# Order of outputs and splitting of inputs in the shared-key attention stage of a decoder kernel

## The reference

```python
def _L1_attn_ref(x, proj_q, proj_k, proj_v, proj_o):
    Q = jnp.einsum('bnd,hdk->bhnk', x, proj_q)
    K = jnp.einsum('bmd,dk->bmk', x, proj_k)
    V = jnp.einsum('bmd,dv->bmv', x, proj_v)
    logits = jnp.einsum('bhnk,bmk->bhnm', Q, K)
    weights = jax.nn.softmax(logits, axis=-1)
    O = jnp.einsum('bhnm,bmv->bhnv', weights, V)
    Y = jnp.einsum('bhnv,hdv->bnd', O, proj_o)
    return Y
x = x + _L1_attn_ref(_layernorm(x, axis=-1), ...)
```

## Time and profile before

| what | us |
|---|---|
| median of the runs | 1040.63 |
| the profiled execution, its time | 1041.43 |
| its span, first to last instruction | 1039.6 |
| TensorE busy in it (88% of the span) | 915.1 |
| VectorE, ScalarE, GpSimd busy | 669.2, 503.6, 326.6 |
| shared-key stage, from the first instruction to the last before the next stage | 498.0 to 748.4 |
| first scores of the loop | 523.63 |
| the stage after it and the rest | 748.4 to 1039.6 |

### The profile page before, as it was taken

The page is one execution under the profiler, slowest core; times in us unless marked ns, Lnnn a source line. Parts: engine busy times, 40 slices in busy tenths (PEclk is TensorE's granted clock), DMA queues, the critical chain, the costliest instruction groups (busy, mean ns, idle before and its releaser), DMA issues. The chain is left out here.

```text
span 1039.6 us, 13450 instructions
## 1 busy us (share of the span) xinstructions
PE 915.1 (88%) x4354; PEld 506.9 (49%) x4354; DVE 669.2 (64%) x1367; ACT 503.6 (48%) x997; POOL 326.6 (31%) x329
## 2 busy tenths in 40 slices
PE   5888889999999986999688888888897999878996
PEld 2445535333332243567566777677542333344565
DVE  5856659888889534354565555655479999444654
ACT  3886445777777740121254444444312777533421
POOL 7236536100000001365154444445131000015933
PEclk9999989999999995899898888988999999969999
DMA  5040054022228307532300000000010352056200
GB/s 149 1 152 1 0 85 77 1 48 47 48 60 257 103 1 250 221 115 91 112 1 0 1 1 1 1 1 1 21 57 3 116 191 81 1 211 211 82 17 26
DMA packets 41657, 73.83 MB, mean 71 GB/s; under 512 B 8964, under 2 KB 27780, under 8 KB 40436
## 3 DMA queue, kind: packets, MB, share of 16 engines
q1 hardware_dynamic: 36372, 59.68, 18.9%
q0 software_dynamic: 4400, 13.11, 4.0%
q10 hardware_dynamic: 816, 0.17, 0.1%
HBM read 49.67 MB, written 10.49 MB: 58 GB/s over the span
## 5 line engine op out<-in xcount | busy, mean ns | idle before, releaser
L1081 DVE TENSOR_REDUCE c_amx<-PS 128x1 f32<-128x512 f32 x256 | 159.0, 682 | 27.7 <-PE PS L981 27.5
L1174 ACT ACTIVATE c_aE<-PS 128x512 f32<-128x512 f32 x256 | 132.5, 603 | 47.1 <-PE PS L993 46.9
L1861 POOL TENSOR_SCALAR s_Pn<-s_Pr,s_rs 128x512 f32<-128x512 f32 x64 | 100.1, 1567 | 122.3 <-DVE s_rs L1903 122.0
L72 POOL TENSOR_SCALAR rstd<-mv 128x4 f32<-128x4 f32 x8 | 1.9, 232 | 337.8 <-DVE mv L95 337.7
L981 PE MATMUL PS<-c_aKs,c_aQs 99*128 99x512 bf16 x256 | 96.6, 388 | 5.1 <-DMA c_aQs<-area 3.6
L993 PE MATMUL PS<-c_aQs,c_aKs 99*128 99x512 bf16 x256 | 94.5, 380 | 3.5 <-ACT c_aE L1174 2.3
L1894 DVE TENSOR_REDUCE s_mx<-PS 128x1 f32<-128x512 f32 x64 | 44.0, 688 | 82.1 <-PE PS L2005 82.1
L1992 ACT ACTIVATE s_Pr<-PS,s_nmx 128x512 f32<-128x512 f32 x64 | 44.1, 689 | 107.8 <-DVE s_nmx L1896 107.5
L1081 DVE TENSOR_REDUCE h_amx<-PS 128x1 f32<-128x512 f32 x128 | 79.3, 682 | 8.4 <-PE PS L981 8.2
L1174 ACT ACTIVATE h_aE<-PS 128x512 f32<-128x512 f32 x128 | 67.5, 601 | 21.6 <-PE PS L993 21.2
L1004 PE MATMUL PS<-c_aE,c_VB 128*17 128x512 f32 x512 | 67.4, 598 | 0.1
(11 more groups left out here) (495 smaller groups left out, 1994.6 us busy)
## 6 DMA issues: line engine op xcount, KB each, us to landing
area<-in_e_w SPq DMA_DIRECT2D x16, 512.0 KB, 9.9
area<-in_g_w SPq DMA_DIRECT2D x8, 1024.0 KB, 6.7
c_aKs<-area SPq DMA_DIRECT2D x48, 128.0 KB
g_B<-in_g_b SPq DMA_DIRECT2D x1, 4096.0 KB, 14.2
c_aQs<-area SPq DMA_DIRECT2D x48, 64.0 KB
h_aQs<-h_QP SPq DMA_DIRECT2D x48, 64.0 KB
early<-in_ctxT SPq DMA_DIRECT2D x2, 1024.0 KB, 7.0
e_B<-in_e_b SPq DMA_DIRECT2D x1, 2048.0 KB
```

The source lines that it names most:

```text
L1081: dve.tensor_reduce(self.mx[:, qt, j, half:half + 1], PS[:, n % MB, :], AX.X, ALU.max).then_inc(self.max_done, 1)
L1174: act.activation(self.E[kt % 2][:, j, :], PS[:, MB + x % XB, :], ACT.Exp, scale=0.25).then_inc(self.exp_done, 1)
L1861: pool.tensor_scalar(Pn[g % NPB][:, :], Pr[g % NPB][:, :], rs[:, g % NPB:g % NPB + 1], None, ALU.mult).then_inc(pn_ready, 1)
```

## The change

Outputs are issued one step later against the transposes, projections two steps later, and the loop has two more steps. VectorE makes the low part of a finished output last in its step and no longer first. In the head, ScalarE copies the transposed input unsplit (XT); TensorE makes keys, values and the queries of the first unit from unsplit f32 operands, one matmul where there were three, and the values move into the loop's first four steps, a pair of row tiles in each. VectorE copies the high parts of the input and of all query weights, GpSimd makes their low parts, the query weights head by head; VectorE makes the low parts of wo head by head in the first eight steps. The parts of wk and wv are gone.

```diff
-    STEPS = G + 2 * TB + LAG + 1
+    STEPS = G + 2 * TB + LAG + 3
     def output_part(g):
 
-        v, m = divmod(g - LAG, TB)
+        v, m = divmod(g - LAG - 1, TB)
         return v - 1, m
 
     def projection_part(g):
 
-        v, i = divmod(g - LAG - 1, TB)
+        v, i = divmod(g - LAG - 3, TB)
         return v - 2, i
...
     def kv_bank(n):
-        return PS[:, 4 + n % 4, :] if n < B else PS[:, 4 + n % 4, 0:2 * DK].rearrange("p (i c) -> p i c", i=2)
+        return PS[:, 5 + n, :] if n < B else PS[:, 7 - n % 2, 0:2 * DK].rearrange("p (i c) -> p i c", i=2)
...
+    def wq_count(h):
+        return h if h > 0 else H
...
-            pool.wait_ge(wqh_ready, 1)
-            pool.tensor_tensor(wqs[1][:, :, :, :], wq[:, :, :, :], wqs[0][:, :, :, :].bitcast(F32),
-                               ALU.subtract).then_inc(wq_ready, 1)
+            def low_weights(h):
+                pool.tensor_tensor(wqs[1][:, h, :, :], wq[:, h, :, :], wqs[0][:, h, :, :].bitcast(F32),
+                                   ALU.subtract).then_inc(wq_ready, 1)
+
+            def low_input(g):
+                b, k = divmod(g, KD)
+                cols = slice(b * S, (b + 1) * S)
+                pool.wait_ge(xh_ready, g + 1)
+                pool.tensor_tensor(XTs[1][:, k, cols], XT[:, k, cols], XTs[0][:, k, cols].bitcast(F32),
+                                   ALU.subtract).then_inc(xl_ready, 1)
+
+            pool.wait_ge(wh_ready, 1)
+            low_weights(1)
+            for g in range(KD):
+                low_input(g)
+            for h in range(2, H):
+                low_weights(h)
+            low_weights(0)
+            for g in range(KD, KD * B):
+                low_input(g)
...
-            for w, parts in ((wk, wks), (wv, wvs)):
-                dve.tensor_copy(parts[0][:, :, :], w[:, :, :]).then_inc(wh_ready, 1)
+            dve.tensor_copy(wqs[0][:, :, :, :], wq[:, :, :, :]).then_inc(wh_ready, 1)
             dve.tensor_copy(wos[0][:, :, :], wo[:, :, :]).then_inc(wh_ready, 1)
-            dve.wait_ge(wh_ready, 2)
-            for w, parts in ((wk, wks), (wv, wvs)):
-                dve.tensor_tensor(parts[1][:, :, :], w[:, :, :], parts[0][:, :, :].bitcast(F32),
-                                  ALU.subtract).then_inc(w_ready, 1)
-            dve.wait_ge(wh_ready, 3)
-            dve.tensor_tensor(wos[1][:, :, :], wo[:, :, :], wos[0][:, :, :].bitcast(F32),
-                              ALU.subtract).then_inc(w_ready, 1)
             for g in range(KD * B):
                 b, k = divmod(g, KD)
                 cols = slice(b * S, (b + 1) * S)
-                dve.wait_ge(xkvh_ready, g + 1)
-                dve.tensor_tensor(XTs[1][:, k, cols], PS[:, g, :], XTs[0][:, k, cols].bitcast(F32),
-                                  ALU.subtract).then_inc(xkv_ready, 1)
-            for n in range(NKV):
+                dve.wait_ge(xf_ready, g + 1)
+                dve.tensor_copy(XTs[0][:, k, cols], XT[:, k, cols]).then_inc(xh_ready, 1)
+
+            def low_kv(n):
                 high, low = kv_parts(n)
-                dve.wait_ge(xkvh_ready, KD * B + n + 1)
-                dve.tensor_tensor(low, kv_bank(n), high.bitcast(F32), ALU.subtract).then_inc(xkv_ready, 1)
+                dve.wait_ge(kvh_ready, n + 1)
+                dve.tensor_tensor(low, kv_bank(n), high.bitcast(F32), ALU.subtract).then_inc(kv_ready, 1)
+
+            def low_projection(h):
+                dve.wait_ge(wh_ready, 2)
+                dve.tensor_tensor(wos[1][:, h, :], wo[:, h, :], wos[0][:, h, :].bitcast(F32),
+                                  ALU.subtract).then_inc(wo_ready, 1)
+
+            for b in range(B):
+                low_kv(b)
 
...
             low_queries(0)
             for g in range(STEPS):
                 n, qt = divmod(g, TB)
-                v, m = output_part(g - 1)
-                if 0 <= v < UN and m == TB - 1:
-                    low_output(v)
                 if g < G:
                     maximum(g)
                 if 1 <= g <= G:
                     inverse_sum(g - 1)
                 if 0 <= g - LAG - 1 < G:
                     low_transposes(g - LAG - 1)
+                if 1 <= g <= VP:
+                    low_kv(B + g - 1)
                 if qt == 2 and n + 1 < UN:
                     low_queries(n + 1)
-                if (g - LAG - 1) % TB == TB - 1 and (g - LAG - 1) // TB - 2 == H - 1:
+                if g < H:
+                    low_projection(g)
+                v, m = output_part(g - 1)
+                if 0 <= v < UN and m == TB - 1:
+                    low_output(v)
+                if projection_part(g) == (H - 1, TB - 1):
                     take_output(0)
...
-            act.activation(wqs[0][:, :, :, :], wq[:, :, :, :], ACT.Copy).then_inc(wqh_ready, 1)
             for g in range(KD * B):
                 b, k = divmod(g, KD)
                 act.wait_ge(xT_done, g + 1)
-                act.activation(XTs[0][:, k, b * S:(b + 1) * S], PS[:, g, :], ACT.Copy).then_inc(xkvh_ready, 1)
-            for n in range(NKV):
+                act.activation(XT[:, k, b * S:(b + 1) * S], PS[:, g, :], ACT.Copy).then_inc(xf_ready, 1)
+
+            def take_kv(n):
                 act.wait_ge(kv_mm, n + 1)
-                act.activation(kv_parts(n)[0], kv_bank(n), ACT.Copy).then_inc(xkvh_ready, 1)
+                act.activation(kv_parts(n)[0], kv_bank(n), ACT.Copy).then_inc(kvh_ready, 1)
+
+            for b in range(B):
+                take_kv(b)
 
...
+                if g < VP:
+                    take_kv(B + g)
...
-            pe.wait_ge(w_ready, 2)
             for b in range(B):
-                pe.wait_ge(xkv_ready, KD * (b + 1))
+                pe.wait_ge(xf_ready, KD * (b + 1))
                 for k in range(KD):
-                    last = products(PS[:, 4 + b, :], [w[:, k, :] for w in wks], [x[:, k, b * S:(b + 1) * S] for x in XTs],
-                                    k == 0, k == KD - 1)
+                    last = pe.matmul(PS[:, 5 + b, :], wk[:, k, :], XT[:, k, b * S:(b + 1) * S],
+                                     start=(k == 0), stop=(k == KD - 1))
                 last.then_inc(kv_mm, 1)
-            for i in range(0, NT, 2):
-                n = B + i // 2
-                if n >= 4:
-                    pe.wait_ge(xkv_ready, KD * B + n - 3)
+            for k in range(KD):
+                last = pe.matmul(PS[:, 4, :], wq[:, 0, k, :], XT[:, k, 0:S], start=(k == 0), stop=(k == KD - 1))
+            last.then_inc(q_mm, 1)
+
+            def values(i):
+
+                n = B + i
+                pe.wait_ge(kv_ready, n - 1 if i >= 2 else B)
                 for j in range(2):
+                    t = 2 * i + j
                     for k in range(KD):
-                        last = products(PS[:, 4 + n % 4, j * DK:(j + 1) * DK],
-                                        [x[:, k, (i + j) * P:(i + j + 1) * P] for x in XTs], [w[:, k, :] for w in wvs],
-                                        k == 0, k == KD - 1)
+                        last = pe.matmul(PS[:, 7 - n % 2, j * DK:(j + 1) * DK], XT[:, k, t * P:(t + 1) * P],
+                                         wv[:, k, :], start=(k == 0), stop=(k == KD - 1), skip_group_check=True)
                 last.then_inc(kv_mm, 1)
-            pe.wait_ge(xkv_ready, KD * B + NKV)
-            pe.wait_ge(wq_ready, 1)
-            pe.wait_ge(w_ready, 3)
 
             def query_part(n, k):
                 b, h = divmod(n, H)
-                if n >= 1 and k == 0:
+                if k == 0:
                     pe.wait_ge(q_ready, n)
+                    pe.wait_ge(xl_ready, KD * (b + 1))
+                    pe.wait_ge(wq_ready, wq_count(h))
                 last = products(PS[:, 4, :], [w[:, h, k, :] for w in wqs], [x[:, k, b * S:(b + 1) * S] for x in XTs],
                                 k == 0, k == KD - 1)
...
                 pe.wait_ge(q_ready, n + 1)
+                pe.wait_ge(kv_ready, b + 1)
...
                 if m == 0:
+                    pe.wait_ge(kv_ready, B + VP)
                     pe.wait_ge(pt_ready, (n + 1) * TB)
...
                     pe.wait_ge(o_ready, n + 1)
+                    pe.wait_ge(wo_ready, H)
...
-            for k in range(KD):
-                query_part(0, k)
             for g in range(STEPS):
                 n, qt = divmod(g, TB)
                 if g < G:
                     scores(g)
+                if g < VP:
+                    values(g)
```

More of the change, by code:

```diff
@@ L1819, in shared_kv_stage @@
     XTs, KTs, Vs = split("XT", [P, KD, T]), split("KT", [P, T]), split("V", [P, NT, DK])
-    wks, wvs = split("wk", [P, KD, DK]), split("wv", [P, KD, DK])
     QT, OT = ([split(f"{name}{n}", [P, S]) for n in range(2)] for name in ("QT", "OT"))
@@ L1825, in shared_kv_stage @@
     mx, nmx, sm, rs = (sb(n, [P, NPB]) for n in ("mx", "nmx", "sm", "rs"))
-    wqh_ready, wq_ready, wh_ready, w_ready = (sem(n) for n in ("wqh_ready", "wq_ready", "wh_ready", "w_ready"))
```

(8 more changed lines are left out.)

## The result

The changed kernel takes 1006.19 us (median of 4 runs, 1004.0 to 1010.64) against 1040.35 us (1037.04 to 1044.63) for the one before: a ratio of 0.9675, with a 95% interval of 0.9626 to 0.9723, and 34 us less. The forecast was 999 us, 42 us less.

A forecast was written before the change was run, and what follows sets the result against it. TensorE was taken to bound the stage, losing time to waits on VectorE's low transposes and half clock behind them. Gains 28.2 + 13.1 + 2.4 - 1.7 = 42.0 us off 1040.63 gave 999; range 992 to 1004, 8-in-10 992 to 1018.

The forecast's parts named there:

- steps 1 and 2: Each unit's output: new wait of 1.37 us in place of 2.07, clock stays full behind it, unit 11.5 us.
- step 3: The 13 units from the output of head 1 to that of head 14: 148.8 us against 177.0, 28.2 gained.
- steps 4 and 5: Head and first eight loop steps: scores begin 15.5 us earlier, of which 13.1 us stay at head 1's output.
- step 6: Tail, up to the last projection: 13.7 us against 16.06, 2.4 us gained.
- step 7: TensorE resting before the first scores and thinly loaded in two early loop steps: one half-clock stretch, 1.7 us, given back.
- A: First steps: GpSimd's normalisation holds VectorE's low projection weights, 2.9 us a step instead of 1.95, time 1006; chance 0.12.
- B: Units: the clock still falls at each new wait, 13.2 us a unit, time 1020; chance 0.12.
- C: Every unit: clock falls and does not return within the next stretch; slower, 1064 us with three such stretches; chance 0.04.
- D: Head's conversions and small differences collide, or the o_ready wait is as long as the old one; some 1008; chance 0.10.

## Why the prediction was right, and where not

1. *The new wait (steps 1 and 2).* Right. It was to be ended by the low output at about 1.1 to 1.2 us as the view shows idle time. It was, at 1.20 us, and the clock stayed at 1.00 behind it, with 2.20 of 3.40 us busy (forecast 2.3). The kernel with the low output first shows that its place in VectorE's step is the whole cause. A unit took 11.60 us (forecast 11.53).
2. *The 13 units (step 3).* Forecast 28.2 us, measured 24.3 (177.03 - 152.76). Three sizes were off. Taking the first batch's result out was put at 0.5 us; the unit that holds it took 13.75, 2.15 more than the others. The rows of VectorE show the chain: additions, statistics and aggregates stand in front of the next maximum.

```profile
635.51 1.29 DVE L1947 TENSOR_TENSOR X<-X,PS 128x512 f32<-128x512 f32 x2 [0.71 <-PE PS L2034]
636.83 1.41 DVE L91 BATCH_NORM_STATS2 st<-X 128x6 f32<-128x256 f32 x4
638.27 0.38 DVE L95 BATCH_NORM_AGGREGATE mv<-st 128x2 f32<-128x6 f32 x4
638.57 0.66 DVE L1914 TENSOR_REDUCE s_mx<-PS 128x1 f32<-128x512 f32 x1
```

   The run that spreads the statistics confirms it: with the additions alone in one place the pause is 1.05 us. The last unit took 12.12 instead of 10.7, with the one fall of the clock. And 0.07 us more in each of the other units made the rest.
3. *Head (steps 4 and 5).* First scores 9.68 us after the start of the stage (forecast 10.15), the output of head 1 12.55 us earlier (forecast 13.1). The walk to the scores was right. VectorE's four input copies were to be done 6.8 us after the start, behind GpSimd's small differences; they took 4.04 us together, their longest 1.49, and were done after 6.4. The 1 us to spare is there as well: VectorE idles 1.02 us before the low queries.

```profile
502.24 1.63 POOL L1858 TENSOR_TENSOR s_wql<-s_wq,s_wqh 128x256 fp32r<-128x256 f32 x1 [8.28 <-DVE s_wqh L1889]
503.27 4.04 DVE L1895 CAST s_XTh<-XT 128x512 fp32r<-128x512 f32 x4
504.23 2.79 POOL L1865 TENSOR_TENSOR s_XTl<-XT,s_XTh 128x512 fp32r<-128x512 f32 x2 [0.37 <-DVE s_XTh L1895]
509.86 0.69 DVE L1927 TENSOR_TENSOR s_QT0l<-PS,s_QT0h 128x512 fp32r<-128x512 f32 x1 [1.02 <-ACT s_QT0h L1994]
```

   The 0.5 us short at the output lie behind the scores: from them to the output of head 1 passed 28.5 us, where 27.6 were forecast. The Trainium skill (SBUF — State Buffer, section "SBUF: two separate sides") says that a float32 copy within SBUF locks the port that VectorE and GpSimd share, as an instruction with two SBUF inputs does against one of GpSimd that reads SBUF, and that the one that starts first holds it to its end. The trace agrees: 4.67 us for one copy beside the 5.42 us difference, and GpSimd's first small difference, 1.63 us behind the copy of wo.
4. *Tail (step 6).* 2.5 us against 2.4.
5. *Slack (step 7).* One half-clock stretch came, as was given back, but in the last unit and not in the head, where the reason for it lay; that the count came out is luck. It is already in the 24.3 us of point 2, so against the sum the units are 3.9 us short and the head 0.5, the tail is 0.1 over, and the 1.7 given back were not spent a second time: together the 2.6 us between 42.0 and 39.4.
6. *From the stage to the time.* The stage gained 39.4 us between the two first profiles, 2.6 less than the sum of 42.0. The executions differ by 35.3 (1041.43 - 1006.17): 2.9 us lie in front of the stage, 0.3 behind it, and 0.9 around the spans (1.83 and 2.77). Of the 2.9 us, 2.2 are the half clock that the first profile of the kernel before did not have there: from GpSimd's last indirect DMA to the stage it took 5.8 us, and 8.1 in the other three profiles of the two kernels. The other 0.7 had come before that. Nor was the 250.4 us stage a constant. Against the second profile the stage gained 243.2 - 211.0 = 32.2 us, and the time 29.0. The measured 34 us lie between. The step that fell short is the base of step 3: it took 12 falls of the clock in one profile as the kernel's cost, and their number is not fixed (10 in the next). The same goes for the head and the tail, which had one fall less each in the second profile: against it the output of head 1 comes 10.8 us earlier and not 12.55. The timed runs lie between: over the 14 that stood beside the experiments' kernels the mean granted clock was 0.937 to 0.945 and the span 1035.2 to 1043.1 us; the two profiles have 0.937 and 0.945.

*Rivals.* The row that speaks on A is this, with the normalisation of 1.59 us that began at 514.95:

```profile
515.08 0.83 DVE L1904 TENSOR_TENSOR s_wol<-s_wo,s_woh 128x256 fp32r<-128x256 f32 x1
```

A gave 1006 us, which is the measured time, but by luck: its mechanism did not occur. It wanted 2.9 us steps with low projection weights held to the end of the normalisation. The new weights took 0.41 to 0.83 us beside normalisations of 1.56 to 1.59 us; the longest, 1.14, stood beside a difference. The output of head 1 would have been 6.7 us later. So here a tensor-scalar on GpSimd did not hold a VectorE difference for its whole length, against the letter of the rule cited, while GpSimd's differences held copies. Two of the new weights took twice the time of the shortest beside a normalisation, so a shorter hold is not ruled out. B (the clock falls at each wait) is refuted by 0.99 over the units and by the unit of 11.60; C was never near; its counter-argument, that every fall in this stage lasted one stretch, holds in the loop but not in the head, where the kernel before ran from 505.43 to 512.25 at 0.50. D gave 1008, also close to the measured time, but its waits of 1.83 us at o_ready did not come, nor a late first score.

What stays open: why the clock falls behind a wait of 1.8 to 1.9 us in most units (12 and 10 of 13 in the two profiles of the kernel before, 12 with the new head and the old order, 11 with the query part behind the output) and not in all; what stands around it is the same work.

## What to carry to other kernels

Where two engines hand a bank back and forth, look at the place of the releasing instruction in its engine's list before its duration: moving one 0.68 us subtraction from last to first in a step was worth 21 us (1006.19 to 985.05). Of that, 19.8 us lie in the 13 units of the profiles (152.76 to 132.96), the one fall of the clock among them. A wait has two prices, its own length and the granted clock behind it. They can be taken apart: short of removing the wait, spare products in it bought back the second. And count falls of the clock over more than one execution before their number goes into a sum as a constant.

## What the runs showed of the hardware that was not expected

- The same wait, 1.90 us in the same place of the same loop, was followed by half clock in most units and by full clock in others. Behind waits of 1.20 us, in five profiles of four kernels, a fall came nowhere.
- With six spare bf16 products (1.47 us) inside a wait of about 1.8 us the clock stayed at full behind all 14 of these waits.
- One fp32r copy of 128x512 within SBUF took from 0.415 us at the shortest to 4.67 us beside a GpSimd difference of 5.42 us.
